# A transformer layer with attention and routed experts: output stage with longer distances, norm sums in strips, token copies two adds ahead

## The chip, the cores and the metric

The kernel runs on one core of a Trainium2 chip. The metric is the device time of one execution in microseconds (us). The kernel before takes 2495.66 us, the median of three runs (2494.31 to 2499.34).

## The reference

The input x has 4 sequences of 2048 tokens with 256 values each, all float32. Cut to what matters:

```python
x = x + layernorm(attention(layernorm(x)))
x = x + layernorm(ffn(layernorm(x)))

# attention: 16 heads of 16, scores / 4, causal mask with a two-way prefix of 196, softmax, @ w_o.T + b_o
# ffn: 8 experts, the best 2 of softmax(x @ gate_w.T) + gate_b, and one shared expert
h1 = xt @ w1[e].T + b1[e]; h3 = xt @ w3[e].T + b3[e]
a = swiglu(h1 * h3)                 # clipped at 7, sigmoid(1.702 g)
y = a @ w2[e].T + b2[e]
out = sum over the chosen e of weight[e] * y   +   shared(xt)
```

## The kernel before

The work is cut into 16 chunks of 512 tokens (`NCH`, `CH`), each with 4 groups of 128 tokens (`TPC`). A stage is a function of its own with its own semaphores; between two stages all engines meet at a barrier (line 82). Inside a stage every engine has its own program, with a `step` for each chunk, and they wait for one another by semaphores only. An engine works in the order of its program, so a wait holds back all that stands behind it. Most float32 products are made of three products of a high and a low part (`product`, line 305); the high part is copied by ScalarE, the low part is subtracted by VectorE.

- `prepare` splits the weights. GpSimd builds an identity and the mask `heads_of` (four rounds of a fill and two selects), then stores zeros to `guard` (1 MB) and waits for them. This ends the stage.
- `project` measures and normalises x (VectorE statistics, GpSimd inverse root and shift, ScalarE), turns it, multiplies it with the weights of q, k and v and stores them. In the step of chunk c VectorE measures chunk c+2, and ScalarE normalises chunk c+1 ahead of copying the high parts of q and k of chunk c. At the end of TensorE's step four products (line 431) add the squares of q and k over each head into one tile of 32 rows; `bound` (line 491) takes their maximum as the first thing in VectorE's next step.
- `find_maxima` turns these maxima into a flag. The branch behind the flag isn't taken here.
- `attend` works through 16 teams of 4 heads. TensorE waits at its start for `ones_set` (rows of ones beside the keys, line 779), and for the first team's `guard` rows (line 865). SyncE issues the four copies of ones, then the two of guard, then the loads of the next chunks.
- `attention_out` (output stage) turns the context of a chunk, multiplies it with w_o, adds the bias, measures and normalises it, adds x (`residual`, line 1273), measures and normalises again, turns the result back, multiplies it with the router's weights (`router`, six products of 512 columns) and stores both results. `in_steps` writes out three steps, loops over ten, and writes out three. In the step whose residual is chunk c, VectorE does: bias and statistics of c+1, low part of the context of c+2, residual and statistics of c, low part `nt_lo` of the normalised c-1 (line 1252).
- `route` first transposes the logits, [8, 8192], to tokens on partitions in 64 pieces (line 1367), then VectorE picks the two experts of each token in a long chain.
- `experts` runs 16 chunks through the shared expert, while GpSimd scatters the tokens into the order of experts, and then 39 chunks of sorted rows (`NEC` is 55). TensorE's step begins with `turn` of the next chunk (line 294). The rows come into two buffers, `xin[0]` and `xin[1]`. For a routed chunk GpSimd copies the weights and token numbers out of `xin` (`read_tails`, lines 1514 and 1515) and adds the results to `sums` by four indirect DMAs (`add`, line 1525). These wait for the weighed results (line 1680) and for the landing of the two adds before. SyncE may load a buffer again (line 1554) only when its last tails are copied:

```python
sp.wait_ge(token_done, c - NCH - 1)
sp.wait_ge(wgt_done, c - NCH - 1)
sp.dma_start(xin[s][:], rin_ch[c - NCH]).then_inc(x_loaded[s], 16)
```

- `combine` normalises the sums, adds the residual and stores the output.

## Time and profile before

| what | value |
|---|---|
| median of 3 runs | 2495.66 us |
| profiled execution, its span | 2501.52 us, 2499.7 us |
| mean granted TensorE clock | 0.943 |
| busy share of the span: TensorE, ScalarE, VectorE, GpSimd | 87%, 72%, 53%, 27% |
| TensorE waits for rows of sorted tokens (line 294) | 18 times, 48.8 us |
| start of project, max, attend, output stage | 13.96, 206.3, 217.5, 1275.5 us |
| start of route, experts, combine | 1460.4, 1497.0, 2417.7 us |

The span reaches from the first to the last instruction. The shares are means over stages with different limits, so each stage has to be read by itself: which engine has no gaps, and what its gaps wait for. The granted clock is a share of 2.4 GHz; 0.5 is 1.2 GHz.

### The profile page before, as it was taken

Reading aid. Unit: us, or ns where it says so; the run is one execution under the profiler, and the core shown is the slowest. Engines: PE = TensorE matmul, PEld = TensorE weight load, DVE = VectorE, ACT = ScalarE, POOL = GpSimd, SP = SyncE. Lnnn points to the kernel's source line nnn. Section 1 sums busy time; section 2 is a strip of 40 time slices with the busy share of each in tenths; the row PEclk is TensorE's granted clock in tenths of the full one; section 3 lists DMA queues with packets and bytes.
Section 4 is the critical chain, followed back from the end, with each engine's and each line's share of the span. In section 5 each row is a group of like instructions: output and inputs, shape, how many; then the busy total and the mean of one; then the engine's idle time right before and its main releaser. Section 6 shows DMA issues by size and latency. Waiting matters only on the chain. (4 is left out here: it accounts for less than half of the span.)

```text
span 2499.7 us, 37800 instructions
## 1 busy us (share of the span) xinstructions
PE 2164.5 (87%) x14101; PEld 1305.1 (52%) x14101; DVE 1323.4 (53%) x2087; ACT 1789.6 (72%) x2267; POOL 679.0 (27%) x709
## 2 busy tenths in 40 slices
PE   5995999999999999999957738999989999999930
PEld 4872333333333333333335527888877777777720
DVE  4663222222222222222228856988877787778848
ACT  4664999999999999999936625555556555556524
POOL 1111000000000000000003317873356555555531
PEclk9997999999999999999979968999999999999965
DMA  5876655555555555544016618896565665666548
GB/s 186 292 279 166 111 91 89 90 90 90 90 95 95 95 95 94 95 70 69 10 63 206 223 57 298 292 290 224 144 154 136 157 158 131 153 156 161 129 114 314
DMA packets 204202, 365.72 MB, mean 146 GB/s; under 512 B 18680, under 2 KB 141176, under 8 KB 195192
## 3 DMA queue, kind: packets, MB, share of 16 engines
q1 hardware_dynamic: 161040, 299.45, 44.6%
q0 software_dynamic: 34256, 55.20, 11.8%
q10 hardware_dynamic: 8736, 8.78, 1.1%
q8 instruction: 108, 1.77, 0.3%
q14 instruction: 62, 0.51, 0.1%
HBM read 219.81 MB, written 143.42 MB: 145 GB/s over the span
## 5 line engine op out<-in xcount | busy, mean ns | idle before, releaser
L956 ACT ACTIVATE att_prob<-att_scores 128x1024 f32<-128x1024 f32 (+2 forms) x1152 | 1022.7, 1052 | 44.0 <-PE att_scores L908 36.7
L927 PE MATMUL att_out<-att_prob,att_va 128*32 128x512 f32 (+3 forms) x5120 | 592.4, 544 | 14.7 <-DVE att_prob L988 14.7
L908 PE MATMUL att_scores<-att_qs,att_ks 50*128 50x512 f32 (+3 forms) x2560 | 471.3, 434 | 22.0 <-DMA att_qs<-guard 20.5
L908 PEld LDWEIGHTS att_scores<-att_qs,att_ks 50*128 50x128 f32 x2560 | 213.7, 185 | 505.5 <-ACT att_prob L956 429.5
L988 DVE SCALAR_TENSOR_TENSOR att_prob<-att_prob,att_tri 128x512 f32<-128x512 f32 x224 | 144.8, 689 | 614.0 <-ACT att_prob L956 614.0
L1525 POOL DMA_INDIRECT sums<-moe_y,moe_token x156 | 321.9, 2064 | 326.2 <-ACT moe_y L1680 290.5
L1587 PE MATMUL moe_ps<-moe_xt_hi,moe_w_hi 128*128 128x512 f32 x880 | 357.4, 406 | 0.6 <-DVE moe_u L1725 0.6
L1587 PE MATMUL moe_ps<-moe_xt_hi,moe_w_lo 128*128 128x512 f32 x880 | 354.0, 402 | 0.0
L1587 PE MATMUL moe_ps<-moe_xt_lo,moe_w_hi 128*128 128x512 f32 x880 | 352.2, 400 | 0.0
L851 POOL DMA_DIRECT2D ctx_scr<-att_cout x64 | 48.2, 753 | 1002.6 <-DVE att_cout L1006 962.1
L1653 ACT ACTIVATE moe_h<-moe_ps,moe_wb 128x512 f32<-128x512 f32 x220 | 149.0, 678 | 152.3 <-PE moe_ps L1587 145.6
L1725 DVE SCALAR_TENSOR_TENSOR moe_u<-moe_ps,moe_wb,moe_h 128x512 f32<-128x512 f32 x220 | 164.1, 746 | 96.0 <-PE moe_ps L1587 96.0
L927 PEld LDWEIGHTS att_out<-att_prob,att_va 128*32 128x32 f32 x5120 | 111.6, 108 | 189.5 <-issue 98.4
L1587 PEld LDWEIGHTS moe_ps<-moe_xt_hi,moe_w_lo 128*128 128x128 f32 x880 | 170.2, 193 | 36.6
L1587 PEld LDWEIGHTS moe_ps<-moe_xt_lo,moe_w_hi 128*128 128x128 f32 x880 | 170.9, 194 | 34.9
L1587 PEld LDWEIGHTS moe_ps<-moe_xt_hi,moe_w_hi 128*128 128x128 f32 x880 | 171.1, 194 | 34.2 <-DVE moe_u L1725 1.0
L1693 DVE TENSOR_TENSOR moe_w_lo<-moe_wraw,moe_w_hi 128x2048 fp32r<-128x2048 f32 x55 | 126.3, 2297 | 43.3 <-ACT moe_w_hi L1626 43.2
L1661 ACT ACTIVATE moe_sig<-moe_u 128x1024 f32<-128x1024 f32 x55 | 58.5, 1063 | 117.3 <-DVE moe_u L1731 117.3
L1626 ACT ACTIVATE moe_w_hi<-moe_wraw 128x2048 fp32r<-128x2048 f32 x55 | 105.2, 1912 | 48.9 <-DMA moe_wraw<-w_experts 48.9
L305 PE MATMUL moe_psY<-moe_w_hi,moe_a_hi 128*128 128x256 f32 x440 | 123.7, 281 | 5.3 <-DVE moe_a_lo L1746 5.3
L294 PE MATMUL moe_psT<-keep_ident,moe_xin 128*128 128x128 f32 x440 | 62.8, 289 | 74.8 <-DMA moe_xin<-rows_in 48.8
L305 PE MATMUL moe_psY<-moe_w_lo,moe_a_hi 128*128 128x256 f32 x440 | 123.3, 280 | 0.0
(203 smaller groups left out, 3077.6 us busy)
## 6 DMA issues: line engine op xcount, KB each, us to landing
moe_wraw<-w_experts SPq DMA_DIRECT2D x55, 1412.0 KB, 7.7
qk_parts<-proj_qk SPq DMA_DIRECT2D x64, 512.0 KB, 4.0
att_qs<-qk_parts SPq DMA_DIRECT2D x180, 128.0 KB
att_ks<-qk_parts SPq DMA_DIRECT2D x180, 128.0 KB
rows_in<-att_zeros SPq DMA_DIRECT2D x13, 1548.0 KB, 20.4
moe_xin<-rows_in SPq DMA_DIRECT2D x39, 516.0 KB, 4.4
proj_xin<-x SPq DMA_DIRECT2D x16, 512.0 KB, 3.9
v_scr<-proj_va SPq DMA_DIRECT2D x16, 512.0 KB, 3.3
```

Of the source, the lines that this page charges most:

```text
L294: last = nc.tensor.transpose(psum[:, k, j * P:(j + 1) * P], src[:, j, k * P:(k + 1) * P], ident[:])
L305: last = nc.tensor.matmul(psum, left[a][:, k, lsl], right[b][:, k, rsl], start=(i == 0), stop=(i == len(steps) - 1))
L908: last = nc.tensor.matmul(pss[e % SBUFS][:, h, at:at + CH - q0], ks[s][rows, half, kt * P:(kt + 1) * P], qs[s][rows, half, c * CH + q0:(c ...
L927: last = nc.tensor.matmul(pso[k % 2][strip, q0:], va[team % 2][:, kt, strip], prob[u % PBUFS][:, h, at:at + CH - q0], start=(kt == 0), sto ...
L956: nc.scalar.activation(prob[u % PBUFS][:, half * 2:half * 2 + 2, start:], pss[e % SBUFS][:, :, start:], ACT.Exp, scale=HD ** -0.5)\
L988: V.scalar_tensor_tensor(block, block, GREATEST, bcast(mask[:], 1, [P, TEAM, w]), op0=ALU.min, op1=ALU.mult).then_inc(masked, 1)
L1525: pool.indirect_dma_start(out=sums, out_offset=bass.IndirectOffsetOnAxis(token[k % TAILS][:, j:j + 1], 0), in_=y[s][:, j, :], in_offset=No ...
L1587: last = nc.tensor.matmul(psum[f % 2][:], wk(w[s][aa], which, k)[:, f * P:(f + 1) * P], xt[s][bb][:, k], start=(i == 0), stop=(i == 5))
L1626: nc.scalar.activation(w[s][0][:, 0:W13], wraw[s][:, 0:W13], ACT.Copy).then_inc(w_hi[s], 1)
L1653: nc.scalar.activation(h3[f % 2][:], ps3[f % 2][:], ACT.Identity, bias=wb[s][:, FB + f:FB + f + 1]).then_inc(h3_done[s], 1)
L1693: V.tensor_tensor(w[s][1][:, 0:W13], wraw[s][:, 0:W13], w[s][0][:, 0:W13].bitcast(F32), ALU.subtract).then_inc(w_lo[s], 1)
L1725: V.scalar_tensor_tensor(u[:, f], ps1[f % 2][:], wb[s][:, f:f + 1], h3[f % 2][:], ALU.add, ALU.mult).then_inc(u_done[s], 1)
```

## The change

- `prepare`: `heads_of` becomes one mask of 32 columns, so one round on GpSimd in place of four. The router's weights are not split; SyncE waits for their load.
- `project`: the four norm products go to four strips of 32 rows of one tile, each on its own, and stand between the two sides of the next chunk's q and k product. The maximum is taken over 128 rows; it stays first in VectorE's step.
- `find_maxima` and `attend`: the ones are filled as [2, 512] and repeated by the DMA; SyncE issues these copies behind the first queries, in the stage of the maxima. The guard rows of the first team are issued by ScalarE at the start of `attend`.
- `attention_out`: 21 steps, all written out. In step k TensorE projects chunk k-1, turns k, turns back k-4 and routes k-5; VectorE does residual and statistics of k-3, bias and statistics of k-1, low part of k. The normalised tokens are no longer split: the router is eight float32 products with 8 moving columns and the tokens as weights, straight into a PSUM tile of [128, 64, 8].
- `route`: no transposes; it reads that tile.
- `experts`: `read_tails(c + 2)` in place of `read_tails(c + 1)` ahead of `add(c)`, and four buffers for the copies in place of three.

```diff
@@ project, TensorE
+                def norm_sums(n, s):
+                    pe.wait_ge(squared[s], n * 2 + 2)
+                    for m in range(4):
+                        strip = slice(m * STRIP_W, (m + 1) * STRIP_W)
+                        last = nc.tensor.matmul(psT[strip, 0, :], heads_of[:], square[:, m], start=True, stop=True,
+                                                skip_group_check=True)
+                    last.then_inc(summed[s], 1)
...
                     for side in range(2):
+                        if side == 1 and prv is not None:
+                            norm_sums(*prv)
...
-                    if nxt is not None:
-                        pe.wait_ge(lo_done[nxt[1]], nxt[0] + 1)
...
-                    pe.wait_ge(squared[s], n * 2 + 2)
-                    for m in range(4):
-                        last = nc.tensor.matmul(psT[0:2 * H, 0, :], heads_of[:, m], square[:, m],
-                                                start=(m == 0), stop=(m == 3))
@@ attend
-        ones = ph.sb("ones", [GUARD, HALVES, SEQ])
+        ones = ph.sb("ones", [GUARD, CH])
...
+        def load_queries(sp):
+            load_parts(sp, 0, slice(0, 1), first[0], 0)
+            load_values(sp, 0, slice(0, 1), first[0])
+            load_ones(sp)
...
-                load_ones(sp)
-                load_guard(0)
                 for c in range(1, BCH):
                     load_heads(sp, 0, slice(c, c + 1), first[c])
...
             def _(act):
+                load_guard(act, 0)
@@ attention_out
+        PROJECT, NORM, ADD, TURN_BACK, LOGITS = 1, 2, 3, 4, 5
+        STEPS = NCH + LOGITS
...
+                load_context(0)
+                for k in range(STEPS):
+                    if chunk(k + 1):
+                        load_context(k + 1)
+                    if chunk(k - ADD + 2):
+                        load_x(k - ADD + 2)
+                    if chunk(k - ADD):
+                        store(k - ADD)
...
+                for k in range(STEPS):
+                    if chunk(k - ADD):
+                        roots(1, k - ADD)
+                    if chunk(k - PROJECT):
+                        roots(0, k - PROJECT)
...
+                def router(c):
+                    pe.wait_ge(n_kept, c + 1)
+                    for j in range(TPC):
+                        for m in range(KT):
+                            last = nc.tensor.matmul(logits[:, c * TPC + j], nt[c % 2][:, m, j * P:(j + 1) * P],
+                                                    gw[:, m], start=(m == 0), stop=(m == KT - 1))
...
+                for k in range(STEPS):
+                    if chunk(k - PROJECT):
+                        projection(k - PROJECT)
+                    if chunk(k):
+                        turn(k)
+                    if chunk(k - TURN_BACK):
+                        turn_back(k - TURN_BACK)
+                    if chunk(k - LOGITS):
+                        router(k - LOGITS)
...
+                for k in range(STEPS):
+                    if chunk(k - NORM):
+                        first_norm(k - NORM)
+                    if chunk(k):
+                        context_hi(k)
+                    if chunk(k - TURN_BACK):
+                        keep_normed(k - TURN_BACK)
+                    if chunk(k - ADD):
+                        second_norm(k - ADD)
...
+                for k in range(STEPS):
+                    if chunk(k - ADD):
+                        residual(k - ADD)
+                    if chunk(k - PROJECT):
+                        add_bias(k - PROJECT)
+                    if chunk(k):
+                        context_lo(k)
@@ route
-                for t in range(NT):
-                    last = nc.tensor.transpose(psl[:, t], logits[:, t * P:(t + 1) * P], ident[0:E, 0:E])
-                last.then_inc(by_token, 1)
@@ experts
-        TAILS = 3
+        TAILS = 4
...
                 read_tails(NCH)
+                read_tails(NCH + 1)
                 for c in range(NCH, NEC):
-                    if c + 1 < NEC:
-                        read_tails(c + 1)
+                    if c + 2 < NEC:
+                        read_tails(c + 2)
                     add(c)
```

## Rows read from the trace of the kernel before

**Rows 1.** Windows: busy us (instructions) by engine, granted clock, DMA share, GB/s
```profile
core 0: us, PE busy (x) PEld busy (x) DVE busy (x) ACT busy (x) POOL busy (x), PEclk, DMA share, GB/s
1516.00:1774.00 258.00, 258.00 (x1401) 221.97 (x1400) 229.81 (x245) 145.87 (x179) 160.01 (x152) 1.00 0.79 261
1774.00:2360.00 586.00, 536.59 (x2805) 454.53 (x2804) 461.22 (x495) 346.58 (x497) 323.47 (x211) 0.96 0.62 149
```

**Rows 2.** Timeline of the expert stage: start us, us, engine, line; idle before in brackets
```profile
1774.53 1.03 PE L294 MATMUL moe_psT<-keep_ident,moe_xin 128*128 128x128 f32 x8
...
2111.60 2.31 POOL L1525 DMA_INDIRECT sums<-moe_y,moe_token  x1 [9.35 <-ACT moe_y L1680]
2120.09 1.56 POOL L1525 DMA_INDIRECT sums<-moe_y,moe_token  x1 [0.30 <-issue]
2121.08 1.02 POOL L1514 COPY moe_wgt<-moe_xin 128x4 f32<-128x4 f32 x1
2122.29 0.37 SPq L1554 DMA_DIRECT2D moe_xin<-rows_in  x1
2126.24 2.29 POOL L1525 DMA_INDIRECT sums<-moe_y,moe_token  x1 [4.01 <-ACT moe_y L1680]
2126.65 1.09 PE L294 MATMUL moe_psT<-keep_ident,moe_xin 128*128 128x128 f32 x8 [2.48 <-DMA moe_xin<-rows_in]
...
2359.84 1.97 PE L294 MATMUL moe_psT<-keep_ident,moe_xin 128*128 128x128 f32 x8 [2.71 <-DMA moe_xin<-rows_in]
```

**Rows 3.** Timeline of VectorE in the output stage
```profile
1309.10 1.22 DVE L1273 TENSOR_TENSOR out_x<-out_attn,out_xin 128x1024 f32<-128x1024 f32 x1
...
1328.00 1.22 DVE L1273 TENSOR_TENSOR out_x<-out_attn,out_xin 128x1024 f32<-128x1024 f32 x1
1331.10 1.19 DVE L1252 TENSOR_TENSOR out_nt_lo<-out_psN,out_nt_hi 128x1024 fp32r<-128x1024 f32 x1
1332.21 1.28 DVE L1263 TENSOR_TENSOR out_att<-out_psO,out_bias 128x512 f32<-128x512 f32 x2
1336.31 1.23 DVE L1247 TENSOR_TENSOR out_ct_lo<-out_psT,out_ct_hi 128x1024 fp32r<-128x1024 f32 x1 [0.84 <-ACT out_ct_hi L1192]
1337.45 1.21 DVE L1273 TENSOR_TENSOR out_x<-out_attn,out_xin 128x1024 f32<-128x1024 f32 x1
...
1445.21 1.23 DVE L1273 TENSOR_TENSOR out_x<-out_attn,out_xin 128x1024 f32<-128x1024 f32 x1 [1.56 <-ACT out_attn L1206]
```

**Rows 4.** Timeline of the routing stage, VectorE's first instruction
```profile
1466.33 0.69 DVE L1389 TENSOR_REDUCE route_top<-route_psl 128x64 f32<-128x512 f32 x1 [9.20 <-PE route_psl L1367]
```

**Rows 5.** Timeline of the projection stage, one round of its loop
```profile
110.88 2.59 DVE L503 TENSOR_TENSOR proj_qk<-proj_psP,proj_qk 128x1024 fp32r<-128x1024 f32 x2 [3.44 <-ACT proj_qk L460]
115.10 1.02 PE L431 MATMUL proj_psT<-proj_square,keep_heads_of 128*32 128x512 bf16 x4 [0.27 <-ACT proj_square L469]
118.47 2.08 ACT L447 ACTIVATE proj_xn<-proj_xin,proj_shift,proj_rstd 128x256 f32<-128x256 f32 x4 [3.51 <-POOL proj_shift L287]
120.45 1.00 ACT L460 ACTIVATE proj_qk<-proj_psP 128x1024 fp32r<-128x1024 f32 x1
121.48 1.23 DVE L503 TENSOR_TENSOR proj_qk<-proj_psP,proj_qk 128x1024 fp32r<-128x1024 f32 x1 [3.35 <-ACT proj_qk L460]
```

**Rows 6.** Timeline and one window (columns as in Rows 1) where attention starts
```profile
217.49 3.20 SPq L779 DMA_DIRECT2D att_ks<-att_ones  x4
220.74 2.52 SPq L865 DMA_DIRECT2D att_qs<-guard  x2
227.25 1.65 PE L908 MATMUL att_scores<-att_qs,att_ks 50*128 50x512 f32 x6 [20.45 <-DMA att_qs<-guard]
...
218.00:224.00 6.00, 0.00 (x0) 0.00 (x0) 5.32 (x6) 0.00 (x0) 3.60 (x5) 0.50 0.11 22
```

**Rows 7.** Timeline of GpSimd in the first stage
```profile
3.03 0.19 POOL L232 TENSOR_SCALAR_AFFINE_SELECT keep_heads_of<-keep_heads_of 128x8 bf16<-128x8 bf16 x1
...
5.93 0.75 POOL L238 DMA_DIRECT2D guard<-prep_zeros  x1 [0.31 <-POOL keep_heads_of L232]
```

338 lines of the change are left out of this document (128 added, 210 removed).

## The prediction

> **What bounds the kernel now.** I first read the page for the share of each engine, then cut the span by windows at the borders of the stages, then read the timeline of each stage that the change touches. The reader is to see that there is no single bound. Attention (1040 us) is bound by ScalarE and the change touches only its start, so what starts earlier there moves the whole rest. The experts have two phases: with the shared expert TensorE is busy 258.00 of 258 us at clock 1.00, with the sorted rows 536.59 of 586 us at 0.96 [rows 1], although a chunk has the same products in both. Projection and output stage have loops through several engines, and there the timeline tells which loop closes last.
>
> **Experts.** Follow one turn of the loop [rows 2]. An add starts at 2111.60, its last DMA is issued at 2120.09, the tails are copied at 2121.08, only then is the buffer loaded (2122.29), and TensorE, which had waited 2.48 us, turns the rows at 2126.65. The wait is not for the transfer but for GpSimd, whose tail copy stands behind an add. Between the turns at 1774.53 and 2359.84 lie 35 chunks: 585.31 us, 16.72 a chunk. The shared phase needs 258.00 us for 1401 matmuls, 80 a chunk (48 of 512 columns, 24 of 256, 8 transposes): 14.7 us a chunk; by the starts of its turns, which lose nothing to missing records, 14.62. The two adds at 2111.60 and 2126.24 are 14.64 apart as well, so routed chunks can keep this pace.
>
> With the copy two chunks ahead, the load of chunk c+4 hangs on the add that now holds up c+3. From that add's start to the turn lie 2126.65 - 2111.60 = 15.05 us in both orders, but the turn it serves is due one chunk, 14.62 us, later. The turn was late by 2.5 us, and it becomes about 12 us early. What is late next? The add itself: it waits for the landing of the one before. From 2111.60 to the last issue are 8.49 us, and the trace shows 3.8 to 6.4 us from an issue to its landing (median 4.4), so 12.3 to 14.9 us; at 2126.24 ScalarE's result came last, not the landing. I take 14.65 a chunk: 35 x (16.72 - 14.65) = 72.5 us. The last turn runs at half clock (1.97 against 1.03 us), and the chunk behind it loses some 1.7 us of clock by the difference of the chunk times; half of that I count, 0.5 to 1.7. **Experts: 73 us**, bounds 60 (14.9 and a wait of 0.1 each) and 75.
>
> **Output stage.** VectorE's period is 1337.45 - 1328.00 = 9.45 us [rows 3]: residual and statistics 3.10 (to 1331.10), `nt_lo` 1.11 (to 1332.21), bias, statistics and a wait of 0.84 up to the low part at 1336.31 (4.10), low part 1.14. The change takes `nt_lo` (1.11) off VectorE. The 0.84 us is a wait for ScalarE's copy, behind TensorE's turn, behind the projection. In the new order residual and statistics stand ahead of the bias, so projection (3.1 us warm), turn (1.0) and copy (1.0) have 6.3 us of VectorE's work to hide behind. New period: 9.45 - 1.11 - 0.84 = 7.50. TensorE has 3.1 + 2 x 1.0 + router; ScalarE 4.1 for two norms and 1.9 for two copies. Both stay below 7.5 if the router needs no more than 2.4 us. The trace has no float32 product of this form. From below, the 64 transposes of [8, 128] of the routing stage took 5.80 us at half clock, 0.09 each; from above, the transposes of this stage, 0.13 each, which load 128 x 128 tokens too. A float32 product appears as two instructions (the count of matmuls in attention says so), so 16 x 0.045 to 16 x 0.13 = 0.7 to 2.1 us, against six products of 512 columns before (1.3 us). I take 1.5; it hides. The transfers are the same 2 MB a chunk at 222 GB/s before, 281 then; the shared phase of the experts moves 261 GB/s on average and 296 in its first part without a stall.
>
> The start. Steps 1 to 4 I take at half clock, as the first steps before, in which TensorE idled 2.4 to 7.9 us ahead of each projection: a projection took 5.3 us there, with a turn 1.4, copy 1.0, low part 1.2 and handovers 9 to 9.8 us a step. But the first step no longer has ScalarE's first norm ahead of the second copy. I get the first residual at 1304.2, 4.9 us ahead of 1309.10, one more slow step of 9.3, one more of 9.2, then 11 steps of 7.45. With 2 us for a dip of the clock, chunk 15's low part ends at 1406.5. Then residual 13 and bias 15 (6.3 us), residual 14 (3.1), and residual 15 waits for GpSimd's root (1.9) and ScalarE's norm (2.1): 1417, against 1445.21 before. Behind it came 15.2 us of serial work; now root, norm, turn, copy and router, 13.6. The stage ends at about 1430.5 against 1460.4. **Output stage: 30 us**, bounds 22 (period 8.0 by the transfers) and 35 (warm from step 3 on, no dip).
>
> **Routing stage.** VectorE's first instruction starts at 1466.33 and waited for the transposes [rows 4]; the stage starts at 1460.4. **5.8 us**, minus up to 0.5 if the load of the gate's bias, needed 4.2 us into the stage, is then late.
>
> **Projection.** It looks like TensorE: 39.16 of 40 us busy in its middle. The norm products take 1.02 us and wait 0.27 [rows 5]. In strips they may run beside one another, as the four strips of values in attention do (eight instructions in 1.06 us, 512 columns each), so about 0.3 us. That makes TensorE faster by 1.0 us a chunk. But a second loop closes just as late [rows 5]: VectorE's low parts at 110.88, low part of x, statistics, GpSimd's root, ScalarE's norm at 118.47 (it had waited 3.51 us for GpSimd), the copy at 120.45, and the next low part at 121.48: 10.60 us, with no gap that TensorE could close. The mean period over chunks 1 to 14 is 10.74. So 13 x 0.14 = 1.8 us in the loop, and 1.1 us at the end, where nothing is measured any more and TensorE alone paces. The maximum waits first in VectorE's step now, with the low part queued behind it: side 0 of the product ends 2.9 us into TensorE's step, sums and maximum take 0.3 + 0.7 (1.0 + 0.7 if the strips run one after another), the low part is due at 6.9. Hidden. **Projection: 2.9 us**, bounds 1.5 and 4.
> The Trainium skill ("TensorE: Matmul & The Clock Gate", Measured speedup vs the span model) says that tiles packed side by side take about as long as one. By that the products would cost 0.25 us in place of 1.02, and a reader who counts only this would expect some 16 us from this edit. This trace agrees on the packing and not on the gain.
>
> **First stage.** The zeros of guard are issued at 5.93, the first of four mask rounds ends at 3.22 [rows 7]; one round leaves the DMA at about 3.5. The weights' loads then still run. **2.0 us**, bounds 1.0 and 2.4.
>
> **Start of attention.** SyncE issues ones at 217.49 and guard at 220.74, TensorE starts at 227.25 [rows 6]. In between the queues move 22 GB/s: each copy of ones fills two partitions with 16 KB each, one copy after another, some 1.3 us each, 5.2 together, and guard stands behind them in the same queue. Now guard is first in ScalarE's queue. First packets 1.4 us after the issue, 1.9 us of transfer, 1.3 to land: 4.6 after the stage's start in place of 9.76, so 5.1 us. Against it: SyncE now issues the ones inside the maxima's stage, which GpSimd ended at 211.2. GpSimd's fill shrinks from 3.5 to 0.5 us; SyncE is done at 209.5 plus 4 issues of 0.42 to 0.80, so 211.2 to 212.7. I take +0.5. **Start of attention: 4.6 us**, bounds 3 and 5.2.
> The Trainium skill ("DMA: Bandwidth & Descriptors", Issuing engines are not separate DMA queues) says that issuing from several engines saves only the sequencer's time. By that the move of guard would save no more than the 3.25 us between SyncE's issues of ones and guard. The window shows why I go beyond it: the ones' transfers leave the path too.
>
> **Sum.** 2.0 + 2.9 + 4.6 + 30 + 5.8 + 73 = 118.3 us off the profiled 2501.52 us: 2383.2. The runs' median lies 5.86 us below the profiled execution, so 2377.
>
> **The rivals.**
> (a) The chain of adds paces the experts. An add's four DMAs and its landing, 12.3 to 14.9 us, are near 14.62. If it takes 15.5 with its handover, 35 x 0.85 = 30 us are lost: 2407. For it: the third DMA of some adds takes 3.23 us, and at the full pace every add may meet VectorE so. Against: the pair 14.64 us apart. Chance 0.1.
> (b) The output stage keeps its period, by the transfers or a half-clock TensorE that the new distances don't cure: 13 x 1.95 = 25 us lost, 2402. For it: 0.68 DMA share at 222 GB/s becomes 0.86. Against: 0.79 and more in the shared phase with TensorE never idle. Chance 0.1.
> (c) Projection follows TensorE: 14 x 1.0 in place of 1.8, 12 us more gain, 2365. Against: the closed loop above. Chance 0.06.
> (d) Slower than before. The adds' chain grows beyond the old pace: every one of the four DMAs takes 3.23 us as the third does now, 13.8 us with the gaps, plus 6.4 to land, 20.2 a chunk: 39 x (20.2 - 16.72) = 136 us lost against 45 gained elsewhere, about 2585. It decides from 17.9 us an add; the trace shows at most 14.9. Chance 0.03.
> (e) The copy ahead doesn't release the load, because it now waits for rows that come late itself: no gain in the experts, 2450. Rows of chunk c+2 are loaded long before the add of c-1 ends. Chance 0.03.
> The forecast itself, 2362 to 2392, has 0.68.
>
> **How the numbers follow.** The terms' bounds add to 94 to 124 us: 2372 to 2402. They won't all fall on one side, but rivals (a) and (b) reach to 2407 and (c) to 2365. The range 2362 to 2404 leaves out 0.2 at most. This kernel's runs spread by 0.2%, about 5 us; a smaller difference is no difference. Only (d) ends above it: faster 0.96, same 0.01, slower 0.03.
>
> **What would show it.** Turns of the experts 14.6 to 14.7 us apart with no wait for sorted rows, clock 1.00, adds still idle for ScalarE's results. Residuals 7.4 to 7.5 us apart from about chunk 2 on, with no wait ahead of the low part. Projection still 10.6, with a gap of some 0.7 us in TensorE. Attention's first product 4.6 us after the stage's start, with the guard packets ahead of the keys'. The prediction is wrong if an add waits for a landing, if TensorE's step in the output stage exceeds 7.5 us, or if unrolled steps or new places in the queues delay a stage's start.

## The result and the profile after

The changed kernel takes 2378.02 us (median of 4 runs, 2377.52 to 2378.7) against 2496.16 us before (2494.31 to 2499.34): ratio 0.9526, 95% interval 0.9509 to 0.9542. The prediction was 2377 us, in a range of 2362 to 2404. The profiled execution took 2377.52 us with a span of 2375.8.

This is the span of each profiled execution cut at the first DMA issue (or first instruction) of each stage; "start" is attention up to its first product. The lower rows are the experiments, told below. A row is one profile. What the same code differs by from row to row is the measure for a small difference: the projection takes 186.6 to 188.1 us in the seven kernels that have the changed one, the output stage 156.3 to 159.5 us in eight, the old routing stage 36.5 to 37.7 us in three, and maxima and start together 20.5 to 21.1 us in four kernels with the old order and 17.1 to 17.9 us in six with the new one.

| us | first | projection | maxima | start | attention | output | routing | experts | combining |
|---|---|---|---|---|---|---|---|---|---|
| before | 13.96 | 192.37 | 11.16 | 9.75 | 1048.29 | 184.91 | 36.51 | 920.70 | 82.07 |
| changed | 11.98 | 186.74 | 13.28 | 4.32 | 1046.06 | 158.29 | 30.23 | 845.31 | 79.58 |
| tails_alone | 13.93 | 193.14 | 10.93 | 9.57 | 1045.69 | 185.95 | 37.70 | 846.49 | 80.95 |
| sums_alone | 12.10 | 187.31 | 11.13 | 9.94 | 1046.70 | 185.92 | 37.24 | 916.46 | 81.02 |
| output_alone | 14.10 | 193.31 | 10.93 | 9.80 | 1045.59 | 158.62 | 30.24 | 910.78 | 79.44 |
| sums_serial | 13.98 | 192.91 | 13.17 | 4.29 | 1045.84 | 159.53 | 30.17 | 844.27 | 79.27 |
| stats_early | 12.00 | 183.22 | 13.51 | 4.28 | 1046.78 | 157.00 | 30.13 | 844.19 | 81.20 |
| values_light | 11.95 | 193.53 | 13.30 | 4.55 | 1047.14 | 156.32 | 30.23 | 844.41 | 79.30 |
| near | 11.74 | 187.34 | 13.10 | 4.64 | 1046.69 | 243.69 | 30.22 | 845.33 | 79.04 |
| fill3 | 11.99 | 186.58 | 12.93 | 4.16 | 1046.60 | 152.90 | 30.09 | 844.16 | 82.64 |
| ones_split | 12.06 | 186.70 | 11.88 | 4.77 | 1046.63 | 159.50 | 30.22 | 844.55 | 79.48 |
| ones_late | 12.01 | 187.05 | 9.87 | 7.48 | 1046.72 | 158.54 | 30.23 | 845.24 | 78.98 |
| start_old | 11.63 | 188.05 | 10.01 | 10.00 | 1047.17 | 157.20 | 30.23 | 844.45 | 79.01 |
| all_three | 11.70 | 183.54 | 12.22 | 4.58 | 1046.26 | 153.10 | 30.25 | 845.45 | 82.75 |

**Experts.** Two windows of the changed kernel, the shared phase and the sorted rows, as in [rows 1]:

```profile
core 0: us, PE busy (x) PEld busy (x) DVE busy (x) ACT busy (x) POOL busy (x), PEclk, DMA share, GB/s
1470.00:1728.00 258.00, 258.00 (x1403) 221.78 (x1402) 230.44 (x245) 146.22 (x179) 164.83 (x155) 1.00 0.79 263
1728.00:2296.00 568.00, 545.89 (x2978) 470.23 (x2977) 485.15 (x523) 361.02 (x525) 367.10 (x228) 0.98 0.66 158
```

Its timeline, the rows that answer to [rows 2] (start, length, engine, line; idle before in brackets):

```profile
1728.30 1.03 PE L293 MATMUL moe_psT<-keep_ident,moe_xin 128*128 128x128 f32 x8
...
1989.75 0.36 SPq L1515 DMA_DIRECT2D moe_xin<-rows_in  x1
...
1993.71 2.28 POOL L1485 DMA_INDIRECT sums<-moe_y,moe_token  x1 [4.02 <-ACT moe_y L1641]
...
2002.17 1.56 POOL L1485 DMA_INDIRECT sums<-moe_y,moe_token  x1 [0.30 <-issue]
...
2003.14 1.03 POOL L1474 COPY moe_wgt<-moe_xin 128x4 f32<-128x4 f32 x1
...
2004.37 0.36 SPq L1515 DMA_DIRECT2D moe_xin<-rows_in  x1
...
2006.08 1.04 PE L293 MATMUL moe_psT<-keep_ident,moe_xin 128*128 128x128 f32 x8
...
2240.00 1.03 PE L293 MATMUL moe_psT<-keep_ident,moe_xin 128*128 128x128 f32 x8
```

The copy still stands behind an add, but the load that it lets go (2004.37) serves the turn one chunk later; the turn at 2006.08 reads rows whose load was issued at 1989.75, 16.3 us earlier. No turn waits for rows any more. From 1728.30 to 2240.00 lie 35 chunks, 14.62 us each (16.72 before), at a granted clock of 1.00. The add waits for ScalarE's result (4.02 us), not for the landing of the add before: from the start of an add to its last landing pass about 12.2 us in both kernels (12.9 at most in the changed one), under the 14.62. The last turn runs at full clock now, 1.03 in place of 1.97 us.

The waits alone are not the whole of what was lost before. Of the 73.6 us by which 35 chunks were longer than 14.62 us each, 48.8 are TensorE's 18 waits for rows; in the other 24.8 TensorE was busy, for the same work, at a lower clock (0.96 over the stretch). A chunk without any wait, behind one that waited, took 16.28 us at a granted clock of 0.90:

```profile
2161.02:2177.30 16.28, 16.28 (x81) 13.86 (x82) 10.22 (x11) 7.69 (x10) 7.96 (x6) 0.90 0.74 205
```

With the waits both parts went: over the 35 chunks of the changed kernel TensorE never idles and the granted clock is 1.00.

**Output stage.** VectorE's residuals, as in [rows 3], with the low parts ahead of some; then windows of a quick step, a slow step and the tail:

```profile
1291.10 1.22 DVE L1248 TENSOR_TENSOR out_x<-out_attn,out_xin 128x1024 f32<-128x1024 f32 x1
...
1338.33 1.21 DVE L1248 TENSOR_TENSOR out_x<-out_attn,out_xin 128x1024 f32<-128x1024 f32 x1
1339.57 1.40 DVE L263 BATCH_NORM_STATS2 out_stats<-out_x 128x6 f32<-128x256 f32 x4
...
1341.42 1.25 DVE L1236 TENSOR_TENSOR out_att<-out_psO,out_bias 128x512 f32<-128x512 f32 x2
...
1344.56 1.19 DVE L1222 TENSOR_TENSOR out_ct_lo<-out_psT,out_ct_hi 128x1024 fp32r<-128x1024 f32 x1
1345.67 1.22 DVE L1248 TENSOR_TENSOR out_x<-out_attn,out_xin 128x1024 f32<-128x1024 f32 x1
...
1350.29 0.69 DVE L1236 TENSOR_TENSOR out_att<-out_psO,out_bias 128x512 f32<-128x512 f32 x1 [0.87 <-PE out_psO L304]
...
1403.14 1.23 DVE L1248 TENSOR_TENSOR out_x<-out_attn,out_xin 128x1024 f32<-128x1024 f32 x1 [1.90 <-ACT out_attn L1191]
```

```profile
1338.33:1345.67 7.34, 6.54 (x56) 6.45 (x56) 6.98 (x22) 5.98 (x11) 3.86 (x9) 1.00 0.93 283
1345.67:1353.97 8.30, 8.08 (x56) 7.99 (x56) 7.07 (x21) 5.39 (x10) 3.86 (x9) 0.79 0.99 320
1403.14:1420.67 17.53, 14.94 (x71) 14.75 (x70) 3.01 (x9) 6.85 (x11) 1.74 (x5) 0.50 0.25 91
```

In the quick step VectorE has no gap. It takes 7.34 us where a step took 9.45: 1.11 us went with `nt_lo` and 0.84 with the wait for ScalarE's copy. In the slow step the granted clock is 0.79, TensorE needs 8.08 us for the same work, and VectorE waits 0.87 us for the second half of the projection. Steps at 0.79 or 0.80 start at the residuals of 1291, 1299, 1315, 1346 and 1376. The tail is at 1.2 GHz throughout (clock 0.50), as its timeline shows on TensorE and ScalarE:

```profile
1407.79 3.42 PE L1159 MATMUL logits<-keep_gw,out_nt 128*128 128x8 f32 x16
1411.08 1.97 PE L293 MATMUL out_psN<-keep_ident,out_xn 128*128 128x128 f32 x8
1412.84 6.84 PE L1159 MATMUL logits<-keep_gw,out_nt 128*128 128x8 f32 x32
1413.08 1.02 ACT L1185 ACTIVATE out_nt<-out_psN 128x1024 f32<-128x1024 f32 x1 [2.06 <-PE out_psN L293]
```

ScalarE has the last chunk's normed rows ready at 1414.1, but the router of chunk 14 still runs (3.42 us from 1412.84), and then chunk 15's needs as long.

**Projection**, one round of its loop, as in [rows 5], a window of its middle, and the row of the kernel before that [rows 5] leave out, ScalarE's second copy of the same round:

```profile
102.80 0.40 PE L402 MATMUL proj_psT<-proj_square,keep_heads_of 128*32 128x512 bf16 x4
...
103.65 2.08 ACT L449 ACTIVATE proj_xn<-proj_xin,proj_shift,proj_rstd 128x256 f32<-128x256 f32 x4 [3.84 <-POOL proj_shift L286]
...
105.64 1.91 ACT L462 ACTIVATE proj_qk<-proj_psP 128x1024 fp32r<-128x1024 f32 x2
...
106.67 2.36 DVE L505 TENSOR_TENSOR proj_qk<-proj_psP,proj_qk 128x1024 fp32r<-128x1024 f32 x2 [2.61 <-ACT proj_qk L462]
```

```profile
60.00:160.00 100.00, 96.96 (x578) 79.05 (x577) 65.63 (x121) 63.89 (x88) 16.41 (x40) 1.00 0.85 299
```

```profile
111.18 1.02 ACT L460 ACTIVATE proj_qk<-proj_psP 128x1024 fp32r<-128x1024 f32 x1 [0.34 <-PE proj_psP L305]
```

The four products in strips take 0.40 us together (1.02 to 1.04 before, one after another). Before, ScalarE's second copy of queries and keys waited 0.34 us for TensorE (0.50 in the next round), and VectorE's second low part waited for this copy. Now the two copies stand close together and the two low parts take 2.36 us in place of 2.59: the wait, which lay inside the loop, is gone. Low part to low part is 10.44 us on average (10.75 before).

**Start of attention**, as in [rows 6]:

```profile
201.91 3.50 SPq L774 DMA_DIRECT2D att_ks<-att_ones  x4
...
212.00 0.77 ACTq L835 DMA_DIRECT2D att_qs<-guard  x2
216.32 1.65 PE L910 MATMUL att_scores<-att_qs,att_ks 50*128 50x512 f32 x6 [16.96 <-DMA att_qs<-guard]
```

**Routing**, as in [rows 4]:

```profile
1420.71 0.69 DVE L1349 TENSOR_REDUCE route_top<-logits 128x64 f32<-128x512 f32 x1 [14.38 <-PEq L83]
```

VectorE begins with the stage itself (1420.67), no transposes ahead of it.

### The profile page after: what moved, and what is told of

It is laid out like the page before. It is cut to its first block and busy times, and to the rows that moved or that the text cites. A ratio compares the mean times of both kernels' runs of the same rounds, so it can differ in the third digit from the quotient of the medians.

```text
span 2375.8 us, 37728 instructions
## 1 busy us (share of the span) xinstructions
PE 2127.9 (90%) x14197; PEld 1307.5 (55%) x14197; DVE 1303.1 (55%) x2070; ACT 1776.9 (75%) x2250; POOL 700.5 (29%) x700
## 5 line engine op out<-in xcount | busy, mean ns | idle before, releaser
L1485 POOL DMA_INDIRECT sums<-moe_y,moe_token x156 | 346.3, 2220 | 224.7 <-ACT moe_y L1641 189.1
L1548 PE MATMUL moe_ps<-moe_xt_hi,moe_w_hi 128*128 128x512 f32 x880 | 347.4, 395 | 0.0
L1548 PE MATMUL moe_ps<-moe_xt_hi,moe_w_lo 128*128 128x512 f32 x880 | 347.0, 394 | 0.0
L1548 PE MATMUL moe_ps<-moe_xt_lo,moe_w_hi 128*128 128x512 f32 x880 | 345.3, 392 | 0.0
L1548 PEld LDWEIGHTS moe_ps<-moe_xt_lo,moe_w_hi 128*128 128x128 f32 x880 | 165.7, 188 | 33.9
L1548 PEld LDWEIGHTS moe_ps<-moe_xt_hi,moe_w_hi 128*128 128x128 f32 x880 | 165.7, 188 | 32.4
L1629 ACT ACTIVATE moe_a_hi<-moe_a 128x1024 fp32r<-128x1024 f32 x55 | 58.4, 1061 | 91.6 <-DVE moe_a L1703 91.6
```

The costliest lines, as they stand in the source:

```text
L1485: pool.indirect_dma_start(out=sums, out_offset=bass.IndirectOffsetOnAxis(token[k % TAILS][:, j:j + 1], 0), in_=y[s][:, j, :], in_offset=No ...
L1548: last = nc.tensor.matmul(psum[f % 2][:], wk(w[s][aa], which, k)[:, f * P:(f + 1) * P], xt[s][bb][:, k], start=(i == 0), stop=(i == 5))
```

## The experiments

Each ratio is taken against runs of the kernel before. Where an experiment's interval overlaps that of the changed kernel, the total tells nothing, and the text goes by the stage that the edit touches, one profile each, measured by what the same code differs by (above, under the result).

### The parts one by one

**tails_alone**: the kernel before, with this alone.

```diff
-        TAILS = 3
+        TAILS = 4
...
                 read_tails(NCH)
+                read_tails(NCH + 1)
                 for c in range(NCH, NEC):
-                    if c + 1 < NEC:
-                        read_tails(c + 1)
+                    if c + 2 < NEC:
+                        read_tails(c + 2)
                     add(c)
```

> The kernel before with one edit: the token copies of the experts two chunks ahead, in rings of four. If the copy behind the add was the whole wait, the experts alone take 845 us as in the changed kernel (921 before), turns 14.62 us apart, and the time is 2496 - 75 = 2421 us. If other parts of the change carry some of it (the rival), the experts lie between 850 and 920 us. The combining stage shrank by 2.4 us in the changed kernel, which nobody had counted: if the experts' new end does that, it is 79.6 us here too, else 82.0.

Measured: 2424.93 us against 2498.94, ratio 0.9707 (0.969 to 0.9723), experts 846.49 us. TensorE has no wait for rows any more. The copy behind the add was the whole wait, and its move needs no other part of the change. The rival falls.

**sums_alone**: the kernel before, with the strips, the new place of the sums and the maximum first in VectorE's step.

```diff
-                    for m in range(4):
-                        last = nc.tensor.matmul(psT[0:2 * H, 0, :], heads_of[:, m], square[:, m],
-                                                start=(m == 0), stop=(m == 3))
+                    for m in range(4):
+                        strip = slice(m * STRIP_W, (m + 1) * STRIP_W)
+                        last = nc.tensor.matmul(psT[strip, 0, :], heads_of[:], square[:, m], start=True, stop=True,
+                                                skip_group_check=True)
```

> The kernel before with the sums of the norms alone changed: strips, their place between the two halves of TensorE's step, the maximum first in VectorE's. The projection took 186.7 us in the changed kernel and 192.4 before, and I had counted 2.9 us, not 5.6. If the edit itself gives it, the projection is 186.7 us here and the time some 6 us under before, 2490. If the earlier end of the first stage or another part of the change gave the rest (the rival), the projection is about 189.5 here.

Measured: 2490.32 us, ratio 0.9964 (0.9943 to 0.9985), with runs from 2476.7 to 2497.1; projection 187.31 us, first stage 12.10. So the edit itself gives 5.1 us in the projection, or up to 6.0 against the two other kernels with the old one (193.1 and 193.3), and the missing mask rounds 1.9 us in the first stage.

**output_alone**: the kernel before, with the output stage, the float32 router and the routing stage of the changed one.

```diff
+        PROJECT, NORM, ADD, TURN_BACK, LOGITS = 1, 2, 3, 4, 5
...
+                        for m in range(KT):
+                            last = nc.tensor.matmul(logits[:, c * TPC + j], nt[c % 2][:, m, j * P:(j + 1) * P],
+                                                    gw[:, m], start=(m == 0), stop=(m == KT - 1))
```

> The kernel before with the output stage, the float32 router and the routing stage of the changed kernel, nothing else. If the parts add up, the output stage takes 158 us (185 before) and routing 30.2 us (36.5 before): 2496 - 33 = 2463 us. Rival: the output stage gained from the earlier parts (its transfers or TensorE's clock at its start), then it is above 162 us here. If its new stores are what shortens the combining stage, that is 79.6 us here and 82.0 us with the tails alone.

Measured: 2457.11 us, ratio 0.9851 (0.9817 to 0.9885). Output 158.62 and routing 30.24 us, as in the whole change; the rival falls. The time is 6 us lower than expected, and that is not in these stages: the experts, whose code is that of before, took 910.78 us here, 916.46 with the sums alone and 920.70 before. With the copy two ahead they take 844.2 to 846.5 in all eleven kernels that have it. So in the old order the stage's time also drifts by some 10 us, and in the new one it does not. The whole runs point the same way: without the new order the executions of one kernel spread by 15.5 us (2489.9 to 2505.4, the kernel before), 20.3 us (sums_alone) and 16.8 us (output_alone), with it by 2.8 us (tails_alone), 1.2 us (changed) and at most 9.2 us (all_three). So the three profiles can't tell whether the 10 us come from the edits or from one execution to the next; what moves the time was not tried. The combining stage is 79 to 83 us without relation to any edit.

### Projection: what paces it

**sums_serial**: the changed kernel, the four products accumulated one after another, in the new place.

```diff
                 def norm_sums(n, s):
                     pe.wait_ge(squared[s], n * 2 + 2)
                     for m in range(4):
-                        strip = slice(m * STRIP_W, (m + 1) * STRIP_W)
-                        last = nc.tensor.matmul(psT[strip, 0, :], heads_of[:], square[:, m], start=True, stop=True,
-                                                skip_group_check=True)
+                        last = nc.tensor.matmul(psT[0:2 * H, 0, :], heads_of[:, m], square[:, m],
+                                                start=(m == 0), stop=(m == 3))
```

> The changed kernel with the four products of the norm sums accumulated one after another again (about 1.0 us in place of 0.4), but in the new place. Theory: the closed loop through VectorE, GpSimd and ScalarE held a wait of ScalarE for TensorE (0.3 to 0.5 us between the two copies of queries and keys), and it goes only if TensorE's step gets shorter: with serial products 0.2 to 0.3 us of it come back each chunk, and the projection takes 190 to 192 us. Rival: the place alone does it (the maximum no longer behind the values' copy), and the projection stays at 187 to 188 us.

Measured: projection 192.91 us, 0.9 above the expected range, all of the gain gone; 2384.76 us in all, ratio 0.9552 (0.9534 to 0.957). The place alone gives nothing; the first stage's 13.98 us is that of before, since the mask rounds are back. A window of this run's projection:

```profile
60.00:160.00 100.00, 99.27 (x564) 79.19 (x563) 66.92 (x127) 62.96 (x84) 14.71 (x36) 1.00 0.84 295
```

TensorE is busy 99.27 of 100 us: with serial products in this place it is the bound.

**stats_early**: the changed kernel, VectorE's statistics ahead of the low parts of queries and keys.

```diff
                     if prv is not None:
                         bound(*prv)
+                    if after(n):
+                        measure(n + 1, s)
                     for side in range(2):
...
                     if nxt is not None:
                         lo(*nxt)
-                    if after(n):
-                        measure(n + 1, s)
```

> The changed kernel with one move in the projection: VectorE takes the statistics of the chunk two ahead before the low parts of queries and keys and not behind the low part of x; it waits there for ScalarE anyway. Theory: a loop of VectorE, GpSimd and ScalarE closes as late as TensorE, and it holds 1.1 us of low part and 1.9 of statistics that this move takes out; then TensorE loses its wait of 0.33 us a chunk for ScalarE's squares, the period goes from 10.43 to 10.1 us and the projection from 186.7 to about 182.5 us. Rival: TensorE alone paces and the wait for the squares stays, since ScalarE waits for TensorE's products: within 1 us of 186.7.

Measured: projection 183.22 us, 3.5 less; 2373.99 us in all, ratio 0.9511 (0.9489 to 0.9533). (all_three, with the same edit, has 183.54.) Its window, and TensorE's and ScalarE's waits in it (us in total, times, longest):

```profile
60.00:160.00 100.00, 99.26 (x598) 81.72 (x597) 69.80 (x130) 66.33 (x89) 16.41 (x40) 1.00 0.90 310
```

```profile
PE proj_psP L304 <- ACT proj_square L471: 0.3, 2, 0.2
...
ACT proj_qk L462 <- PE proj_psP L304: 33.7, 20, 2.3
```

TensorE's wait for the squares (3.0 us in 9 times in the same window of the changed kernel) is 0.3, and it is ScalarE that waits now, for TensorE. The period is 10.1 us: TensorE's own.

**values_light**: the changed kernel with a third of the values' products, so that TensorE has time to spare.

```diff
-                        last = product(nc, psP[2][:, j * D:(j + 1) * D], xt[s], wqkv, slice(j * P, (j + 1) * P),
-                                       slice(2 * D, 3 * D))
+                        for k in range(KT):
+                            last = nc.tensor.matmul(psP[2][:, j * D:(j + 1) * D], xt[s][0][:, k, j * P:(j + 1) * P],
+                                                    wqkv[0][:, k, 2 * D:3 * D], start=(k == 0), stop=(k == KT - 1))
```

> The changed kernel, leaving out of the values' products both with a low part (8 matmuls of 256 columns in place of 24 a chunk), so TensorE has 1.9 us less a chunk; the values are then only rounded products. By the closed loop (low parts 2.27, low part of x 1.13, statistics 1.85, root 2.1, norm 2.0, copy 1.0 = 10.4 us) the period stays at 10.4 us and the projection at 183 to 186 us. Rival: TensorE paces, period 8.5, projection 156 us.

Measured in a single run: projection 193.53 us, outside what either expected. Three low parts of x in a stretch at full clock, and two windows:

```profile
69.33 1.21 DVE L489 TENSOR_TENSOR proj_xt_lo<-proj_psT,proj_xt_hi 128x1024 fp32r<-128x1024 f32 x1
...
79.71 1.22 DVE L489 TENSOR_TENSOR proj_xt_lo<-proj_psT,proj_xt_hi 128x1024 fp32r<-128x1024 f32 x1
...
90.17 1.21 DVE L489 TENSOR_TENSOR proj_xt_lo<-proj_psT,proj_xt_hi 128x1024 fp32r<-128x1024 f32 x1
```

```profile
60.00:100.00 40.00, 32.79 (x176) 25.49 (x176) 26.22 (x52) 25.06 (x36) 6.54 (x16) 1.00 0.83 286
100.00:120.00 20.00, 16.06 (x67) 11.82 (x68) 12.33 (x25) 11.54 (x17) 3.27 (x8) 0.83 0.83 301
```

With TensorE busy 32.79 of 40 us the period is 10.38 and 10.46 us, that of the changed kernel: the loop through VectorE, GpSimd and ScalarE closes by itself at 10.4 us. That part of the expectation holds, and TensorE's pace as the only bound falls. What nobody expected: TensorE idles in every round here, and from 100 to 120 us the granted clock is 0.83, where the periods are 11.4 to 11.8 us; in the same stretch of the changed kernel it is 1.00. Four other rounds of this run, outside the windows shown, are as long (11.5 to 11.8 us). The stage is 6.8 us longer than in the changed kernel, with less work on TensorE.

### Output stage: distances and clock

**near**: the changed kernel with shorter distances. What ran has the first norm one step nearer as well (second number), which the text of its expectation leaves out.

```diff
-        PROJECT, NORM, ADD, TURN_BACK, LOGITS = 1, 2, 3, 4, 5
+        PROJECT, NORM, ADD, TURN_BACK, LOGITS = 1, 1, 2, 3, 4
```

> The changed kernel with the adds, the turning back and the router one step nearer (2, 3, 4 in place of 3, 4, 5), everything else the same. The residual then stands right behind the statistics of its own chunk's bias: root 1.9 and norm 2.1 us lie open, and VectorE has 1.1 us of low part to cover them. Theory: period 7.34 + 4.0 - 1.1 = 10.2 us, output stage 158 + 13 x 2.9 - one step of 7 = 188 us or more, about 2408 us in all. Rival: the gain came from the work taken off VectorE (1.11 us of low part), not from the distance: period 8.3, output stage about 170, 2390 us.

Measured: 2463.8 us, ratio 0.988 (0.9853 to 0.9908), output stage 243.69 us: far beyond both. One round of it, on VectorE, GpSimd and ScalarE:

```profile
1368.85 1.22 DVE L1248 TENSOR_TENSOR out_x<-out_attn,out_xin 128x1024 f32<-128x1024 f32 x1
...
1375.88 0.38 DVE L268 BATCH_NORM_AGGREGATE out_mv<-out_stats 128x2 f32<-128x6 f32 x4
...
1376.46 0.23 POOL L276 TENSOR_SCALAR out_std<-out_mv 128x4 f32<-128x4 f32 x1 [2.44 <-DVE out_mv L268]
...
1378.35 2.08 ACT L1191 ACTIVATE out_attn<-out_att,out_shift,out_rstd 128x256 f32<-128x256 f32 x4 [7.80 <-POOL out_shift L286]
1380.33 1.00 ACT L1179 ACTIVATE out_ct_hi<-out_psT 128x1024 fp32r<-128x1024 f32 x1
...
1381.37 1.22 DVE L1222 TENSOR_TENSOR out_ct_lo<-out_psT,out_ct_hi 128x1024 fp32r<-128x1024 f32 x1 [5.10 <-ACT out_ct_hi L1179]
1382.51 1.22 DVE L1248 TENSOR_TENSOR out_x<-out_attn,out_xin 128x1024 f32<-128x1024 f32 x1
```

The period is 13.66 us. With the norm in the step of its own bias, ScalarE stands at the norm first and waits 7.80 us for the root; the context's copy is behind it on ScalarE, and VectorE's low part waits 5.10 us for the copy. So all of it lies in a row: 7.03 us of residual, bias and statistics (to 1375.88; 0.90 of them are a wait for the projection on TensorE, whose granted clock is 0.75 here), 2.47 to ScalarE's start, 1.98 of norm, 1.04 of copy, 1.14 of low part. The stage is 85 us longer than in the changed kernel and 59 us longer than in the kernel before, though `nt_lo` is off VectorE here too: taking this work off VectorE gives nothing where the norm isn't a step behind its statistics. What the longer distance of the adds alone is worth, the question that the expectation asks, this run doesn't tell; with the norm left at 2 it wasn't tried and stays open.

**fill3**: the changed kernel with filler on TensorE.

```diff
+        FILL = 3
...
+                def fill():
+                    for _ in range(FILL):
+                        nc.tensor.matmul(psF[:], wo[0][:, 0, 0:P], wo[0][:].rearrange("p k d -> p (k d)"),
+                                         start=True, stop=True)
...
                     if chunk(k - LOGITS):
                         router(k - LOGITS)
+                    if chunk(k):
+                        fill()
```

> The changed kernel with three products of 512 columns more in each of the first 16 steps of the output stage's TensorE, into a bank of their own that nobody reads (0.64 us at full clock, in the 0.81 us that TensorE waits for the low part). In the changed kernel the granted clock is 1.00 in most steps and 0.79 in every third or fourth, and those take 8.2 to 8.5 us in place of 7.34. Theory: the dips follow TensorE's gap, and without it they go: 4 steps by 1.0 us, and some of the cold start, output stage 152 to 154 us (158.3). Rival: they come anyhow, and each slow step gets 1.3 us longer: 163 us.

Measured: output stage 152.90 us, 5.4 less, in the expected range; 2373.01 us in all, ratio 0.9504 (0.9479 to 0.9529). Against all eight kernels with the same stage but for the filler it is 3.4 to 6.6 us less. The dips didn't all go: counted from low part to low part, three steps of 8.3 to 8.5 us are left of fifteen, where the changed kernel has seven above 8.2. The first two are 7.0 and 7.2 us in place of 9.4 and 8.6, and these two are 3.7 of the gain. In all_three, with the same filler, the first step takes 9.1 us again, and of the others only one is above 8 us (8.1). That slow steps come with TensorE's gaps is supported, that filling the gaps removes them all is not.

### Start of attention

**ones_split**: the changed kernel, two of the four copies of ones issued by ScalarE behind the keys.

```diff
-            load_ones(sp)
+            load_ones(sp, 0)
...
             load_parts(act, 0, slice(0, 1), first[0], 1)
+            load_ones(act, 1)
```

> The changed kernel with the four copies of ones issued half by SyncE and half by ScalarE, in the stage of the maxima. That stage grew from 11.16 to 13.28 us, where I had counted 0.5. Theory: SyncE's four issues, 3.50 us up to 205.4, are what ends last, and the stage ends 6.6 us behind them; with half the stage is 1.7 us shorter, 11.6. Rival: the stage ends when its transfers are through (the next stage's instructions come in only then), and it stays at 13.3 us.

Measured: maxima 11.88 us (1.4 less), the start 0.45 longer; 2377.17 us in all, ratio 0.9524 (0.9502 to 0.9547), which can't be told from the changed kernel. The maxima's stage is near the expected 11.6, so SyncE's issues did set its end.

**ones_late** and **start_old**: the changed kernel with the ones issued in attention again, guard first in ScalarE's queue (ones_late) or behind the ones in SyncE's (start_old).

```diff
         def load_queries(sp):
             load_parts(sp, 0, slice(0, 1), first[0], 0)
             load_values(sp, 0, slice(0, 1), first[0])
-            load_ones(sp)
...
             def _(sp):
...
+                load_ones(sp)
+                load_guard(sp, 0)          (start_old only)
                 for c in range(1, BCH):
...
                 def _(act):
-                load_guard(act, 0)         (start_old only)
```

> The changed kernel with the four copies of ones issued by SyncE in attention's first instructions again, guard still first in ScalarE's queue. From the start of the maxima's stage to attention's first product it took 20.9 us before and 17.6 after. If the ones' transfers were what the start waited for, the maxima's stage is 11.1 us and the first product comes 8 to 9.5 us into attention: 19 to 20.6. Rival: only guard's place behind the ones counted, the first product comes 4.3 to 5 us in, 15.4 to 16, better than the changed kernel.

> As the run with the ones late, and guard behind them in SyncE's queue as in the kernel before; what is left of the change there is the smaller tile of ones, read eight times over. Theory: 11.1 us and 9.7 us, as before, 20.9 in all. Rival: the copies from the smaller tile are shorter, and the first product comes 1 us or more earlier.

From the start of the maxima to the first product, in us: before 20.91, start_old 20.01, ones_late 17.35, changed 17.60, ones_split 16.65. The kernels start_old and ones_late ran once each. The rows of ones_late:

```profile
208.92 3.52 SPq L774 DMA_DIRECT2D att_ks<-att_ones  x4
208.93 0.76 ACTq L834 DMA_DIRECT2D att_qs<-guard  x2
216.41 0.79 PE L910 MATMUL att_scores<-att_qs,att_ks 50*128 50x512 f32 x2 [16.71 <-DMA att_ks<-att_ones]
```

The first product does wait for the ones there, 7.48 us into attention, a little less than the 8 to 9.5 expected; but the maxima's stage is 3.4 us shorter than in the changed kernel. The sum, 17.35, lies between the two expectations (19 to 20.6, and 15.4 to 16) and among the kernels with the ones issued early (17.1 to 17.9): their early issue only moves its cost. Guard's new place gives 2.7 us (20.01 to 17.35), with the ones now the last to come. The smaller tile with GpSimd's shorter fill gives 0.9 (20.91 to 20.01), between the theory of start_old and its rival, and not much more than the 0.6 by which the old order differs from kernel to kernel.

### A version that beats both

**all_three**: the changed kernel with the edits of stats_early, ones_split and fill3, and more filler in the output stage's last steps.

```diff
+        TAIL_FILL = {0: 8, 1: 8, 2: 6}
...
+                    fill(FILL if chunk(k) else TAIL_FILL.get(k - NCH, 0))
```

> The changed kernel with the statistics early (projection 183.2 us alone), the copies of ones from two engines, the filler of three products in the output stage (152.9 us alone), and more filler in its last steps (8, 8 and 6 products), where TensorE stands at half clock and the routers of chunks 14 and 15 take 3.42 us each. If the tail gets warm, its two routers take 1.85 us each and the turning 1.04 in place of 1.97: the output stage is 148 us, and the whole 3.5 + 1 + 10 under the changed kernel, 2363 us. Rival: in the tail TensorE waits too long and stays at 1.2 GHz, then the filler costs what it takes and the stage is 153 to 156 us.

Measured over 5 runs: 2367.16 us, ratio 0.9469 (0.9449 to 0.949), under the whole interval of the changed kernel (0.9509 to 0.9542), but 4 us above the expected 2363. Output stage 153.10 us and not 148: the filler of the tail gave nothing. Its tail on TensorE:

```profile
1392.25 2.10 PE L1169 MATMUL out_psF<-keep_wo_hi 128*128 128x512 f32 x8
1396.94 1.97 PE L293 MATMUL out_psN<-keep_ident,out_xn 128*128 128x128 f32 x8 [2.59 <-ACT out_xn L1201]
1398.70 3.42 PE L1163 MATMUL logits<-keep_gw,out_nt 128*128 128x8 f32 x16
1401.98 2.91 PE L1169 MATMUL out_psF<-keep_wo_hi 128*128 128x512 f32 x6
```

TensorE still waits 2.59 us, then turns at 1.97 us, the half clock; and the six products behind the router take 2.91 us there. The rival's reading holds.

## Why the prediction was right, and where its terms were off

The mechanism of each large part held; that the total came within 1 us of the forecast is luck, as the last paragraph of this section shows. Term by term, by the prediction's own steps:

- **Experts**, 73 predicted, 75.4 by the profiles, 74.0 by tails_alone's medians. The load moved ahead, no landing became the next wait, 14.62 us a chunk and not 14.65, and the last turn ran at full clock. The 75.4 lie 0.4 above the term's bound of 75. The prediction told of the loss as a wait; a third of it, 24.8 of 73.6 us, was TensorE at a lower clock, which is in its sum because it took the whole difference of the chunk times. Rivals (a), (d) and (e) didn't come.
- **Output stage**, 30 predicted, 26.6 measured, in its bounds. Up to residual 15 the estimate is within a microsecond: 140.8 us into the stage (1403.14 - 1262.38) against 141.5 (1417 less 1275.54, where the stage began before). The period is 7.34 (7.50), the first residual came 28.7 us into the stage as forecast, the slow first steps are 8.4 and not 9.3, and the dips cost some 3.3 us where 2 were allowed. The whole shortfall is the step behind: "root, norm, turn, copy and router, 13.6" is 17.5. The two routers of chunks 14 and 15 take 3.42 us each at half clock, one behind the other; I had taken one at 1.5, and the turn ahead of it takes 1.97 us. The kernel before had shown this clock: its last turns took 1.9 us too. Rival (b) didn't come. At full clock the router takes 1.85 us, in the bounds 0.7 to 2.1.
- **Routing**, 5.8 predicted, 6.3 measured, 0.5 above the bound; the old stage takes 36.5 to 37.7 us in three kernels, so this is no more than the difference between kernels.
- **Projection**, 2.9 predicted, bounds 1.5 and 4, measured 5.6 (5.1 with the sums alone): the one term clearly outside its bounds. The step that failed is "10.60 us, with no gap that TensorE could close". The loop does close (values_light: 10.4 us with TensorE 82% busy), but the 2.59 us of two low parts in [rows 5] hold a wait of ScalarE for TensorE between its two copies, 0.3 to 0.5 us. With it gone the period is 10.44 and not the forecast 10.6, and TensorE's gap is 0.3 us and not 0.7: 14 times 0.31 (10.75 - 10.44) is 4.3 us, and about 1.3 at the end. Rival (c), 12 us more than forecast, came to 2.7 of them. sums_serial shows that it took TensorE's shorter step, and stats_early that TensorE stands only 0.3 us behind the loop. A group of two instructions was read as one length of work. The Trainium skill ("TensorE: Matmul & The Clock Gate", Measured speedup vs the span model) has tiles packed side by side take about as long as one. The trace agrees: the four strips take 0.40 us together, and one of the four products of before is 0.38 us long. The 0.25 and 0.3 us of the prediction were a quarter of the 1.02, which is the distance from one product to the next and not the length of one. The 16 us that a reader would count from the rule were not there.
- **Start of attention**, 4.6 predicted, 3.3 measured, in its bounds. The first product came 4.32 us in, where 4.6 was forecast. Off was the price: the maxima's stage grew by 2.1 and not by 0.5, since SyncE's four issues took 0.87 us each on average and ended 6.7 us into the stage, where GpSimd had been the last at 4.8. The 0.5 was taken near the lower end of 0.42 to 0.80 us an issue, though [rows 6] have 3.20 us for four of them, which alone makes it 1.5. "The ones' transfers leave the path too" is right for attention's own start and worth nothing in the sum (ones_late). The move of guard alone gives 2.7 us. The Trainium skill ("DMA: Bandwidth & Descriptors", Issuing engines are not separate DMA queues) has an issue from another engine save only the sequencer's time, by the rows 3.25 us. The 2.7 agree with it, and no run shows more; but as the ones came last in ones_late, none shows what the move would give without them.
- **First stage**, 2.0 predicted, 1.98 measured. sums_alone shows it to be the mask rounds.

The measured terms add to 119.2 us, the predicted ones to 118.3: 2.7 too little for the projection, 2.4 for the experts and 0.5 for the routing, against 3.4 too much for the output stage and 1.3 for the start. The profiles differ by 124.0 us. The other 4.7 are attention (2.2) and the combining stage (2.5), where the change does nothing. In the twelve other profiles attention takes 1045.6 to 1047.2 us with the old start as with the new, so 1048.3 is the profiled execution of before, not an effect; its time lay 5.4 us above its median, and the prediction had taken 5.86 off for that. So the total is a sum of errors of both signs, and nearer than the terms are. The terms' own bounds, added up, give 93 to 127 us, 2368 to 2403 us, and not the 94 to 124 of the prediction; the range doesn't hang on it.

## What to carry to other kernels

Where two loops close within 3% of each other, look for each inside the other before you price an edit of one: a group's length in the timeline may hold a wait for the very engine that the edit makes faster. Sum a stage's tail at the clock that the tail shows before the change, and count what is queued on TensorE ahead of the last product. Where a wait goes, look at the granted clock behind it too: a third of what the waits of the experts cost stood there. When the distances of a software pipeline change, follow each engine's own order, for one instruction that waits at the head of a queue puts everything behind it into the loop.

## What the runs showed of the hardware

- Four bf16 products into four strips of 32 columns, each moving 512, take 0.40 us together; accumulated one after another 1.02 us, each 0.38 us long.
- A float32 router of 16 instructions with 8 columns each takes 1.85 us at full clock and 3.42 at half: its loads of 128 x 128 tokens as weights are busy for all of this time (1.86 us for 16 at full clock).
- With 16 of the values' matmuls left out of each round of the projection (values_light, one run), TensorE was busy 82% of the time in place of 97%, the granted clock was 0.83 from 100 to 120 us in place of 1.00, and the stage 6.8 us longer. Useless products in the output stage made it 5.4 us shorter.
- In the experts before the change, a chunk that followed a wait of 3.2 us took 16.28 us at a granted clock of 0.90; without the waits every chunk takes 14.62 us at 1.00.
- SyncE's issue of one copy of ones takes 0.87 us on average in the form that reads a tile of 512 eight times, at either place (3.50 and 3.52 us for four), and 0.80 in the old form [rows 6].
